# Router weights side by side: two products in place of three for each chunk, and a sum on VectorE

## The chip, the cores and the metric

One core of one Trainium2 chip runs the whole kernel. The metric is the device time of one execution in microseconds (us); lower is better.

## The reference

One decoder layer on 32 sequences of 100 rows with 512 features: self-attention with 16 heads of 128, cross-attention to a context, and a feed-forward layer with a router over 8 experts, of which two add a low-rank term. Only the router matters here. Its logits are the normalised rows times a 512 x 8 matrix:

```python
router_logits = xf @ Wr.T                       # (3200, 512) @ (512, 8)
probs = jax.nn.softmax(router_logits.astype(jnp.float32), axis=-1)
topw, topi = jax.lax.top_k(probs, K)            # K = 2
expert_w = jnp.sum(jax.nn.one_hot(topi, E, dtype=x.dtype) * topw[..., None], axis=1)
...
g_lora = xf @ Ag_e.T @ Bg_e.T * SCALING         # R = 16 columns for each of 8 experts
h = jax.nn.silu(gate_base + g_lora) * (up_base + u_lora)
```

## The kernel before

Products are made in fp16 with split operands. Each fp32 operand is kept as a high half and a low half, and the helper `three` makes one product of three (lines 1553 to 1555): high x high, high x low, low x high, added up in PSUM. Each matmul loads its own stationary operand first (LDWEIGHTS, shown as PEld).

The kernel has a first stage (self-attention, until about 1290 us) in which the weights of the second stage are loaded and split too, in pieces of a fixed order (`B_PIECES`; the router's is number 3 of 17). The second stage goes over groups of five sequences, that is 500 rows in 4 tiles of 125; there are six of them, and a last group of two sequences, 200 rows in 2 tiles of 100. A group has a cross-attention part (`cross_attention`) and a feed-forward part (`layer`), and the order of each engine's work is written out by hand, with semaphores between the engines.

At the end of the cross-attention part of TensorE stand, in this order: the last output products of the group before, the transposes of the normalised rows (`turn_late`, line 1646), the router (`route`), and the low-rank factors (`factors`: 2 x 12 products with as many columns as the group has rows). The layer part follows: `turn_mask` (line 1913) transposes the expert masks, then come the gate and up products in 11 chunks. In the first chunk two more masks are transposed behind the gate products, and the low-rank products wait for the masked factors (`alo`). In the first group nothing stands in front of the router, and three tiles are routed and multiplied by the factors before the fourth is transposed.

In `route` the transposed rows are the stationary operand (125 or 100 columns) and the router's weights are the moving one (8 columns). The results of all tiles of a group lie side by side in one PSUM bank:

```python
for t in range(a, b):
    mm = three(ps[0:tm, 6, t * NE:(t + 1) * NE], [
        (yT_hi[:, e, t * tm:(t + 1) * tm], yT_lo[:, e, t * tm:(t + 1) * tm],
         wr_hi[:, e, :], wr_lo[:, e, :]) for e in range(KC)])
```

On VectorE, `layer` begins with a chain of 16 small instructions (`link`), each of which waits for the one before: the largest logit (line 1459), the subtraction (1460), the first and the second choice (1453 to 1465). Then `spread_out` (1447) writes the first two masks, 16 columns for each expert, four links make the weights, and `spread_out` writes the other two. ScalarE takes two exponentials in between (lines 1004 and 1007; they wait for links 2 and 7). Then VectorE multiplies the factors by the masks (1485, which needs the turned masks of ScalarE, line 1011) and splits the product (1491). Line 1224 is VectorE's half of the split of the transposed rows, which `route` needs.

Of the kernel before, what the change touches and what calls it, by code (L numbers as in the profile page):

```python
# [26 lines left out]
ALU = mybir.AluOpType  # L27
ACT = mybir.ActivationFunctionType
AX = mybir.AxisListType
F32 = mybir.dt.float32  # L30
F16 = mybir.dt.float16
BF16 = mybir.dt.bfloat16

P = 128
S = 100
E = 512
KC = E // P
# [16 lines left out]
NE = 8  # L54
# [51 lines left out]
def decoder_layer(nc, x, wq, wk, wv, wo, q_scale, k_scale, ctxT_in, cwq, cwkv_in, cwo, wg, wu, wd,  # L106
# [8 lines left out]
    with ExitStack() as ctx:  # L115
# [27 lines left out]
        cut = Cut(0)  # L143
# [25 lines left out]
        cut = Cut(w0_at)  # L169
        cwq_hi, cwq_lo = cut([KC, E], F16), cut([KC, E], F16)  # L170
        cwo_hi, cwo_lo = cut([KC, E], F16), cut([KC, E], F16)
        cwkv_hi, cwkv_lo = cut([2 * E], F16), cut([2 * E], F16)
        wr_hi, wr_lo = cut([KC, NE], F16), cut([KC, NE], F16)
        ag_hi, ag_lo = cut([KC, P], F16), cut([KC, P], F16)
        au_hi, au_lo = cut([KC, P], F16), cut([KC, P], F16)
        ad_hi, ad_lo = cut([FC, P], F16), cut([FC, P], F16)
# [12 lines left out]
        cut = Cut(stages_at)  # L189
# [6 lines left out]
        col = {n: cut([NT]) for n in ("m", "d", "r", "m2", "w2")}  # L196
        assert cut.at <= w1_at

        cut = Cut(w1_at)
        yT_hi, yT_lo = cut([KC, GS], F16), cut([KC, GS], F16)  # L200
# [9 lines left out]
        cut = Cut(hb_at + 7687)  # L210
# [11 lines left out]
        cut = Cut(shared_end)  # L222
# [15 lines left out]
        cut = Cut(a_rest)  # L238
# [3 lines left out]
        cut = Cut(hb_at)  # L242
# [217 lines left out]
        def add_piece(src, chunks, width, *parts):  # L460
            B_PIECES.append((src, chunks, width, parts))

        def add_pieces(hi, lo, src, chunks, width):
            step = max(1, 2048 // width)
            src = src.rearrange("(c p) n -> p c n", p=P)
            for a in range(0, chunks, step):
                b = min(chunks, a + step)
                add_piece(src[:, a:b, :], b - a, width,
                          (flat(hi)[:, a * width:b * width], flat(lo)[:, a * width:b * width],
                           0, (b - a) * width))  # L470

        for args in ((cwq_hi, cwq_lo, cwq, KC, E), (cwo_hi, cwo_lo, cwo, KC, E),
                     (cwkv_hi, cwkv_lo, cwkv_in, 1, 2 * E),
                     (wr_hi, wr_lo, wr, KC, NE), (ag_hi, ag_lo, ag, KC, P),
                     (au_hi, au_lo, au, KC, P), (ad_hi, ad_lo, ad, FC, P),
                     (bu_hi, bu_lo, bu, 1, F)):
            add_pieces(*args)
        for hi, lo, w in ((wg_hi, wg_lo, wg), (wu_hi, wu_lo, wu)):
            for e in range(KC):
# [26 lines left out]

            return range(len(B_PIECES))[B_IN_A + b:B_IN_A + b + 1]

        LINKS = 16

        @block.sync
        def _(sp):
# [260 lines left out]
        def _(act):  # L773
# [226 lines left out]
            def layer(g, nb, nxt):  # L1000
                nt, tm = tiles_of(nb)
                gs = nb * S
                act.wait_ge(c["chain"], g * LINKS + 2)
                act.activation(rt["p"][0:tm, 0:nt, :], rt["l"][0:tm, 0:nt, :], ACT.Exp,
                               scale=1 / (X_SCALE * W_SCALE)).then_inc(c["rexp"], 1)
                act.wait_ge(c["chain"], g * LINKS + 7)
                act.activation(col["w2"][0:tm, 0:nt], col["m2"][0:tm, 0:nt], ACT.Exp,
                               scale=1 / (X_SCALE * W_SCALE)).then_inc(c["rexp"], 1)
                def take_mask(k):
                    act.wait_ge(c["mT"], g * 4 + k + 1)  # L1010
                    act.activation(msk[:, k, 0:gs], ps[:, 2 + k % 2, 0:gs],
                                   ACT.Copy).then_inc(c["mTe"], 1)

                take_mask(0)
                take_mask(1)
                for i in range(4):
                    act.wait_ge(c["am"], g * 4 + i + 1)
                    act.activation(am_hi[:, i, 0:gs], tmp[:, i, 0:gs], ACT.Copy).then_inc(c["ahi"], 1)
                    if i % 2:
                        take_mask(2 + i // 2)  # L1020

                def late_hi(k):
                    act.wait_ge(c["late"], 16 * (k + 1 + (k == 2)))
                    for hi, stage, _ in late_parts(k, True):
                        op = act.activation(hi, stage, ACT.Copy, scale=W_SCALE)
                    op.then_inc(c["latehi"], 1)

                def half_h(i, jj):
                    act.wait_ge(c["h"], g * 3 * FC + 3 * jj + i + 1)
                    if i and jj:  # L1030
                        act.wait_ge(c["ad"], g * FC + jj)
                    act.activation(hb_hi[:, jj, 0:gs] if i == 0 else hs_hi[:, i - 1, 0:gs],  # L1032
                                   hh[:, i, 0:gs], ACT.Copy).then_inc(c["hhi"], 1)

                for j in range(FC):
                    act.wait_ge(c["base"], g * 2 * FC + 2 * j + 1)
                    if j:
                        act.wait_ge(c["gs"], g * 2 * FC + 2 * j)
                    act.activation(gb[:, 0:gs], ps[:, 0, 0:gs], ACT.Copy).then_inc(c["gb"], 1)
                    if j:  # L1040
                        act.wait_ge(c["h"], g * 3 * FC + 3 * (j - 1) + 1)
                    act.activation(gate[:, 0, 0:gs], ps[:, 0, 0:gs], ACT.Silu,
                                   scale=1 / (X_SCALE * W_SCALE)).then_inc(c["sg0"], 1)
                    if j:
                        half_h(1, j - 1)
                        half_h(2, j - 1)
                    act.wait_ge(c["base"], g * 2 * FC + 2 * j + 2)
                    if j:
                        act.wait_ge(c["us"], g * 2 * FC + 2 * j)
                    act.activation(ub[:, 0:gs], ps[:, 1, 0:gs], ACT.Copy,  # L1050
                                   scale=H_SCALE / (X_SCALE * W_SCALE)).then_inc(c["ub"], 1)
                    half_h(0, j)
                    for i in (1, 2):
                        act.wait_ge(c["gs"], g * 2 * FC + 2 * j + i)
                        act.activation(gate[:, i, 0:gs], gate[:, i, 0:gs], ACT.Silu,
                                       scale=1 / (X_SCALE * W_SCALE)).then_inc(c["sgs"], 1)
                    if g == 0 and j in LATE_AT:
                        late_hi(LATE_AT[j])
                    if nxt and j == CTX_CHUNK:
                        act.wait_ge(c["alo"], g * 4 + 4)  # L1060
                        context_hi(g + 1, nxt * S)
                half_h(1, FC - 1)
                half_h(2, FC - 1)
                if nxt:
                    cross_attention(g + 1, nxt, nb)
                else:
                    act.wait_ge(c["dsum"], g + 1)
                    act.activation(d_hi[:, 0:gs], tmp[:, 0, 0:gs], ACT.Copy).then_inc(c["dhi"], 1)
# [5 lines left out]
        def _(dve):  # L1074
# [352 lines left out]
            def layer(g, nb, nxt):  # L1427
# [6 lines left out]
                def link(ins):  # L1434
                    ins.then_inc(c["chain"], 1)
                    chain[0] = chain[0] + 1
                    dve.wait_ge(c["chain"], chain[0])

                def wide(name):
                    return col[name][0:tm, 0:nt].unsqueeze(2).to_broadcast([tm, nt, NE])  # L1440

                dve.wait_ge(c["rank"], NE)
                lg, p, a, rest = (rt[n][0:tm, 0:nt, :] for n in "lpab")
                rl = ps[0:tm, 6, 0:nt * NE].rearrange("p (t e) -> p t e", e=NE)

                def spread_out(k):
                    dve.tensor_copy(spread[0:tm, 0:nt, k, :, :],
# [8 lines left out]
                    link(dve.tensor_reduce(col["m"][0:tm, 0:nt], a, AX.X, ALU.max))  # L1456
                    link(dve.tensor_tensor(sel[k][0:tm, 0:nt, :], a, wide("m"), ALU.is_equal))

                link(dve.tensor_reduce(col["m"][0:tm, 0:nt], rl, AX.X, ALU.max))
                link(dve.tensor_tensor(lg, rl, wide("m"), ALU.subtract))  # L1460
                first_of(0, lg)
                link(dve.scalar_tensor_tensor(out=rest, in0=sel[0][0:tm, 0:nt, :], scalar=-1e30,
                                              in1=lg, op0=ALU.mult, op1=ALU.add))
# [82 lines left out]
        def _(pe):  # L1546
            pe.wait_ge(s["ident"], 1)

            def three(out_ap, pairs):

                mm = None
                for i, (ah, al, bh, bl) in enumerate(pairs):
                    pe.matmul(out_ap, ah, bh, start=(i == 0), stop=False)  # L1553
                    pe.matmul(out_ap, ah, bl, start=False, stop=False)  # L1554
                    mm = pe.matmul(out_ap, al, bh, start=False, stop=(i == len(pairs) - 1))  # L1555
                return mm
# [97 lines left out]
            def wide(out_ap, w_hi, w_lo, a, b, gs):  # L1654

                return three(out_ap, [(w_hi[e][:, a:b], w_lo[e][:, a:b],
                                       yT_hi[:, e, 0:gs], yT_lo[:, e, 0:gs]) for e in range(KC)])
# [92 lines left out]
            def cross_attention(g, nb, last_nb):  # L1750
# [117 lines left out]
                def route(a, b):  # L1868

                    mm = None  # L1870
                    pe.wait_ge(c["lnlo"], g * 2 * NT + nt + b)
                    for t in range(a, b):
                        mm = three(ps[0:tm, 6, t * NE:(t + 1) * NE], [
                            (yT_hi[:, e, t * tm:(t + 1) * tm], yT_lo[:, e, t * tm:(t + 1) * tm],
                             wr_hi[:, e, :], wr_lo[:, e, :]) for e in range(KC)])
                    return mm

                def factors(a, b):
# [123 lines left out]
```

## Time and profile before

| | us |
|---|---|
| median of 3 runs | 2565.74 |
| lowest, highest | 2563.83, 2566.78 |
| the profiled execution | 2562.61 |
| its span | 2560.1 |
| TensorE busy (matmuls) | 2459.1 (96%) |
| VectorE busy | 1554.3 (61%) |
| ScalarE busy | 1340.1 (52%) |
| mean granted TensorE clock | 0.981 of 2.4 GHz |

The span runs from the first to the last instruction of the profiled execution; 2.5 us of its time lie around it. An engine's busy time is the union of its instructions. A matmul's own duration contains its latency, so that the sum over matmuls counts time twice where they overlap; the distance between two starts is what one of them costs. The granted clock is what the chip's throttle lets TensorE have: 1.00 is 2.4 GHz, 0.50 is 1.2 GHz.

### The profile page before, as it was taken

How to read it: one execution, taken by the hardware profiler on the slowest of the kernel's cores; microseconds unless marked ns; L12 is line 12 of the kernel's file. 1: busy time of each engine (PE TensorE's matmuls, PEld its weight loads, DVE VectorE, ACT ScalarE, POOL GpSimd, SP SyncE). 2: the span in 40 equal slices, each digit the busy share in tenths (PEclk: the TensorE clock that was granted, in tenths of full speed). 3: DMA queues.
4: the chain of work that ended last, by engine and by line, in shares of the span. 5: the costliest groups of instructions: out<-in, count | busy, mean ns of one | idle time of the engine just before them, and what ended most of it. 6: DMA issues, size and time to landing. Idle time of an engine off the chain costs nothing.

```text
span 2560.1 us, 46046 instructions
## 1 busy us (share of the span) xinstructions
PE 2459.1 (96%) x16474; PEld 1334.5 (52%) x16474; DVE 1554.3 (61%) x3592; ACT 1340.1 (52%) x4109; POOL 844.0 (33%) x794
## 2 busy tenths in 40 slices
PE   6998999999999999999888999999999999999998
PEld 3554554554554555544454465465465465465466
DVE  7777766666566666666545655655655655655644
ACT  4554555555555555565464563563563563564433
POOL 3333333333333333333222422422422422422412
PEclk9999999999999999999969999999999999999999
DMA  5677667777677767798611001001001001001000
GB/s 157 147 175 164 148 151 166 157 166 167 144 164 169 156 154 179 163 187 186 145 63 50 33 18 53 1 18 53 1 18 53 1 17 53 1 18 41 8 17 14
DMA packets 456259, 241.56 MB, mean 94 GB/s; under 512 B 389136, under 2 KB 391824, under 8 KB 455284
## 3 DMA queue, kind: packets, MB, share of 16 engines
q1 hardware_dynamic: 456034, 238.63, 39.8%
q8 instruction: 133, 2.18, 0.4%
q14 instruction: 92, 0.75, 0.1%
HBM read 78.66 MB, written 32.77 MB: 44 GB/s over the span
## 4 chain that ended last, share of the span: by engine, by line
PE 90%; DVE 4%; ACT 3%; issue 2%; POOL 1%; POOLq 0%; ACTq 0%; DVEq 0%
PE ps L1553 25%; PE ps L1555 24%; PE ps L1554 24%; PE ps L1732 3%; PE ps L1733 2%; PE ps L1734 2%; PE ps L1846 2%; ACT mem L974 2%; PE ps L1830 1%; PE ps L1802 1%; PE ps L1742 1%; PE ps L1746 1%; PE ps L1744 1%; PE ps L1824 1%; DVE mem L1224 1%
## 5 line engine op out<-in xcount | busy, mean ns | idle before, releaser
L1553 PE MATMUL ps<-mem 128*128 128x512 f16 (+7 forms) x3992 | 1226.8, 326 | 46.0 <-issue 30.3
L1554 PE MATMUL ps<-mem 128*128 128x512 f16 (+7 forms) x3992 | 1238.2, 325 | 0.0
L1555 PE MATMUL ps<-mem 128*128 128x512 f16 (+7 forms) x3992 | 1222.2, 325 | 0.0
L1553 PEld LDWEIGHTS ps<-mem 128*128 128x128 f16 (+3 forms) x3992 | 413.5, 104 | 372.4 <-issue 51.2
L1555 PEld LDWEIGHTS ps<-mem 128*128 128x128 f16 (+3 forms) x3992 | 414.7, 104 | 316.7 <-issue 9.0
L1554 PEld LDWEIGHTS ps<-mem 128*128 128x128 f16 (+3 forms) x3992 | 416.4, 104 | 305.0 <-issue 8.0
L749 POOL TENSOR_TENSOR mem<-mem 128x500 f32<-128x500 f32 (+1 forms) x231 | 269.2, 1165 | 460.6 <-DVE mem L1505 194.6
L699 POOL TENSOR_TENSOR mem<-mem 128x8 f32<-128x8 f32 x100 | 163.7, 1637 | 510.1 <-DVE mem L1137 510.1
L844 ACT ACTIVATE mem<-ps,mem 100x100 f32<-100x100 f32 x512 | 169.1, 346 | 186.4 <-DVE mem L1167 185.4
L1505 DVE TENSOR_TENSOR mem<-mem 128x500 f16<-128x500 f32 (+1 forms) x231 | 144.7, 650 | 177.0 <-ACT mem L1032 170.8
L711 POOL TENSOR_TENSOR mem<-mem 100x400 f16<-100x400 f32 x128 | 158.5, 1238 | 184.6 <-ACT mem L854 184.6
L824 ACT ACTIVATE mem<-ps 128x512 f32<-128x512 f32 x200 | 117.7, 589 | 169.7 <-DVE mem L1131 85.2
L763 POOL TENSOR_TENSOR mem<-mem 100x400 f32<-100x400 f32 x128 | 107.5, 852 | 290.1 <-DVE mem L1372 290.0
L1032 ACT ACTIVATE mem<-mem 128x500 f16<-128x500 f32 (+1 forms) x231 | 127.9, 585 | 108.2 <-POOL mem L749 108.1
L1198 DVE SCALAR_TENSOR_TENSOR mem<-ps,mem 128x512 f32<-128x512 f32 x100 | 69.0, 690 | 176.3 <-PE ps L1555 176.2
L974 ACT ACTIVATE mem<-ps,mem 100x100 f32<-100x100 f32 x512 | 168.4, 378 | 8.2 <-DVE mem L1351 8.2
L834 ACT ACTIVATE mem<-ps,mem 128x128 f16<-128x128 f32 x400 | 114.0, 368 | 82.8 <-POOL mem L699 82.8
L1131 DVE TENSOR_REDUCE mem<-mem 128x4 f32<-128x512 f32 x200 | 136.1, 681 | 31.6 <-ACT mem L824 31.6
L1516 DVE TENSOR_TENSOR mem<-ps,mem 128x500 f32<-128x500 f32 (+1 forms) x154 | 97.3, 632 | 60.6 <-PE ps L1555 60.2
L705 POOL TENSOR_TENSOR mem<-mem 100x400 f32<-100x400 f32 x128 | 109.1, 852 | 71.9 <-DVE mem L1177 71.9
L1145 DVE SCALAR_TENSOR_TENSOR mem<-ps,mem 128x128 f32<-128x128 f32 x400 | 112.1, 343 | 34.0 <-POOL mem L699 33.8
L974 ACT ACTIVATION_READ_ACCUMULATOR mem<-ps,mem 100x1 f32 x512 | 124.5, 243 | 0.0
(123 smaller groups left out, 3045.5 us busy)
## 6 DMA issues: line engine op xcount, KB each, us to landing
x<-mem SPq DMA_DIRECT2D x100, 256.0 KB, 2.9
mem<-x SPq DMA_DIRECT2D x75, 256.0 KB, 3.7
mem<-in_x SPq DMA_DIRECT2D x50, 256.0 KB, 3.3
mem<-x SPq DMA_DIRECT2D x12, 1000.0 KB
mem<-mem SPq DMA_DIRECT2D x32, 200.0 KB
mem<-mem SPq DMA_DIRECT2D x6, 1000.0 KB
out<-mem SPq DMA_DIRECT2D x6, 1000.0 KB
mem<-in_wq SPq DMA_DIRECT2D x16, 256.0 KB, 4.1
```

The costliest lines, as they stand in the source:

```text
L699: pool.tensor_tensor(rr[:, u % 2, :], ms[:, u % 2, :], half[:, 0:2 * HG], ALU.pow).then_inc(s["rr"], 1)
L711: pool.tensor_tensor(p_split[0:S, n % 2, 1, :, 0:S], probs[0:S, :, :], p_split[0:S, n % 2, 0, :, 0:S], ALU.subtract).then_inc(s["plo"], 1)
L749: pool.tensor_tensor(hh[:, i, 0:gs], gate[:, i, 0:gs], ub[:, 0:gs] if i == 0 else up[:, i - 1, 0:gs], ALU.mult).then_inc(c["h"], 1)
L824: act.activation(sq[:, :, :], bank(kind, u).rearrange("p (h d) -> p h d", d=D), ACT.Square).then_inc(s["sq" + kind], 1)
L844: op = act.activation(probs[0:S, h, :], ps_s[0:S, h * S:(h + 1) * S], ACT.Exp, bias=mx[0:S, h:h + 1], accum_out=den[0:S, h:h + 1])
L974: op = act.activation(cprobs[0:S, i, m, :], ps[0:S, i, m * S:(m + 1) * S], ACT.Exp, bias=cmx[0:S, i, m:m + 1], accum_out=cden[0:S, i, m:m ...
L1032: act.activation(hb_hi[:, jj, 0:gs] if i == 0 else hs_hi[:, i - 1, 0:gs], hh[:, i, 0:gs], ACT.Copy).then_inc(c["hhi"], 1)
L1131: dve.tensor_reduce(ss[:, i, m * HG:(m + 1) * HG], sq[:, :, :], AX.X, ALU.add).then_inc(s["ss"], 1)
L1505: dve.tensor_tensor(lo, hh[:, i, 0:gs], hi, ALU.subtract).then_inc(c["hlo"], 1)
L1553: pe.matmul(out_ap, ah, bh, start=(i == 0), stop=False)
L1554: pe.matmul(out_ap, ah, bl, start=False, stop=False)
L1555: mm = pe.matmul(out_ap, al, bh, start=False, stop=(i == len(pairs) - 1))
```

## The change

The two halves of the router's weights are laid side by side, 16 columns for each chunk. The rows' high half is multiplied by both in one product, the rows' low half by the high half in a second. PSUM then holds two sums of 8 columns for each tile; a new first link on VectorE adds them into `lg`, and the largest logit and the subtraction read `lg` (SBUF) in place of PSUM. The chain has 17 links, and ScalarE waits for one link more. The router's piece keeps its place among the pieces.

```diff
-        wr_hi, wr_lo = cut([KC, NE], F16), cut([KC, NE], F16)
+        wr_both = cut([KC, 2 * NE], F16)
+        wr_hi, wr_lo = wr_both[:, :, 0:NE], wr_both[:, :, NE:2 * NE]
...
-                     (wr_hi, wr_lo, wr, KC, NE), (ag_hi, ag_lo, ag, KC, P),
+                     (ag_hi, ag_lo, ag, KC, P),
...
+            if args[0] is ag_hi:
+                add_piece(wr.rearrange("(c p) n -> p c n", p=P), KC, NE, (wr_hi, wr_lo, 0, KC * NE))
             add_pieces(*args)
...
-        LINKS = 16
+        LINKS = 17
...
-                act.wait_ge(c["chain"], g * LINKS + 2)
+                act.wait_ge(c["chain"], g * LINKS + 3)
...
-                act.wait_ge(c["chain"], g * LINKS + 7)
+                act.wait_ge(c["chain"], g * LINKS + 8)
...
-                rl = ps[0:tm, 6, 0:nt * NE].rearrange("p (t e) -> p t e", e=NE)
+                rl = ps[0:tm, 6, 0:nt * 2 * NE].rearrange("p (t k e) -> p t k e", k=2, e=NE)
...
-                link(dve.tensor_reduce(col["m"][0:tm, 0:nt], rl, AX.X, ALU.max))
-                link(dve.tensor_tensor(lg, rl, wide("m"), ALU.subtract))
+                link(dve.tensor_reduce(lg, rl.rearrange("p t k e -> p t e k"), AX.X, ALU.add))
+                link(dve.tensor_reduce(col["m"][0:tm, 0:nt], lg, AX.X, ALU.max))
+                link(dve.tensor_tensor(lg, lg, wide("m"), ALU.subtract))
...
-                        mm = three(ps[0:tm, 6, t * NE:(t + 1) * NE], [
-                            (yT_hi[:, e, t * tm:(t + 1) * tm], yT_lo[:, e, t * tm:(t + 1) * tm],
-                             wr_hi[:, e, :], wr_lo[:, e, :]) for e in range(KC)])
+                        at = 2 * NE * t
+                        for e in range(KC):
+                            pe.matmul(ps[0:tm, 6, at:at + 2 * NE], yT_hi[:, e, t * tm:(t + 1) * tm],
+                                      wr_both[:, e, :], start=(e == 0), stop=False)
+                            mm = pe.matmul(ps[0:tm, 6, at:at + NE], yT_lo[:, e, t * tm:(t + 1) * tm],
+                                           wr_hi[:, e, :], start=False, stop=(e == KC - 1))
```

## Rows read from the trace of the kernel before

**Rows 1.** The page, busy time of each engine and chain that ended last.

```profile
PE 2459.1 (96%) x16474; PEld 1334.5 (52%) x16474; DVE 1554.3 (61%) x3592; ACT 1340.1 (52%) x4109; POOL 844.0 (33%) x794
...
PE 90%; DVE 4%; ACT 3%; issue 2%; POOL 1%; POOLq 0%; ACTq 0%; DVEq 0%
```

**Rows 2.** TensorE's waits from 1340 us on: total, times, longest.

```profile
PE ps L1553 <- DVE mem L1224: 8.9, 7, 3.3
PE ps L1913 <- DVE mem L1447: 2.5, 2, 1.8
```

**Rows 3.** Timeline of TensorE, group 2: start, length, then the instruction.

```profile
1747.05 0.17 PE L1553 MATMUL ps<-mem 128*125 128x8 f16 x1
...
1749.80 0.37 PE L1553 MATMUL ps<-mem 128*128 128x500 f16 x1
...
1754.88 1.02 PE L1913 MATMUL ps<-mem 125*128 125x125 f32 x8
...
1761.68 0.37 PE L1553 MATMUL ps<-mem 128*128 128x500 f16 x1
```

**Rows 4.** Timeline of VectorE, group 2, with the idle time before.

```profile
1749.97 0.19 DVE L1459 TENSOR_REDUCE mem<-ps 125x4 f32<-125x32 f32 x1 [2.03 <-PE ps L1555]
1750.20 0.19 DVE L1460 TENSOR_TENSOR mem<-ps,mem 125x32 f32<-125x32 f32 x1
...
1752.47 0.76 DVE L1447 COPY mem<-mem 125x512 f32<-125x512 f32 x2
...
1756.61 2.44 DVE L1485 SCALAR_TENSOR_TENSOR mem<-ps,mem 128x500 f32<-128x500 f32 x4 [1.61 <-ACT mem L1011]
1758.96 2.44 DVE L1491 TENSOR_TENSOR mem<-mem 128x500 f16<-128x500 f32 x4
```

**Rows 5.** Group 1: timeline of TensorE; busy times and granted clock (PEclk, third from the end).

```profile
1554.28 0.17 PE L1553 MATMUL ps<-mem 128*125 128x8 f16 x1
...
1557.03 0.37 PE L1553 MATMUL ps<-mem 128*128 128x500 f16 x1
...
1563.79 1.02 PE L1913 MATMUL ps<-mem 125*128 125x125 f32 x8
...
1554.00:1557.40 3.40, 3.40 (x53) 3.08 (x51) 0.88 (x2) 0.00 (x0) 0.00 (x0) 1.00 0.13 42
1557.40:1560.80 3.40, 3.40 (x11) 1.22 (x9) 2.96 (x15) 0.44 (x2) 0.00 (x0) 0.50 0.55 174
```

**Rows 6.** Group 0: timeline of TensorE; one stretch with the granted clock.

```profile
1355.92 0.22 PE L1553 MATMUL ps<-mem 128*125 128x8 f16 x1 [3.26 <-DVE mem L1224]
...
1359.71 0.47 PE L1553 MATMUL ps<-mem 128*128 128x375 f16 x1
...
1362.80 0.36 PE L1554 MATMUL ps<-mem 128*128 128x375 f16 x1
...
1365.07 0.59 PE L1646 MATMUL ps<-mem 125*128 125x125 f32 x4
...
1371.01 1.04 PE L1913 MATMUL ps<-mem 125*128 125x125 f32 x8 [1.76 <-DVE mem L1447]
...
1356.10:1359.50 3.40, 3.40 (x34) 3.40 (x34) 0.22 (x1) 0.00 (x0) 0.00 (x0) 0.50 0.30 128
```

**Rows 7.** Group 6: timeline of TensorE.

```profile
2484.30 0.17 PE L1553 MATMUL ps<-mem 128*100 128x8 f16 x1
...
2485.40 0.25 PE L1553 MATMUL ps<-mem 128*128 128x200 f16 x1
2485.49 0.25 PE L1554 MATMUL ps<-mem 128*128 128x200 f16 x1
...
2488.32 0.53 PE L1913 MATMUL ps<-mem 100*128 100x100 f32 x4 [0.70 <-DVE mem L1447]
```

**Rows 8.** Groups by form, VectorE, reduces: busy, mean ns, idle before.

```profile
L1351 DVE TENSOR_REDUCE mem<-ps 100x4 f32<-100x400 f32 x128 | 66.6, 567 | 64.9 <-PE ps L1830 64.9
...
L1459 DVE TENSOR_REDUCE mem<-ps 125x4 f32<-125x32 f32 x6 | 1.2, 193 | 11.1 <-PE ps L1555 11.1
```

## The prediction

> **What bounds the kernel now.** I read the page first. TensorE is busy 96% of the span and the chain that ended last lies on it for 90% [rows 1]. VectorE is busy 61%: an instruction more on it costs nothing by itself, only where TensorE waits for it. I then asked for TensorE's waits in the stretch that the change touches (1340 us to the end). In seven groups TensorE waited for `spread_out` only twice, 2.5 us in all, and for the row splits of L1224 seven times, 8.9 us [rows 2]. So the router's chain on VectorE is in the open in two groups of seven, and hidden in five. I number the groups 0 to 6; 0 to 5 have four row tiles of 125, and 6 has two of 100. Which is which shows in the timelines of groups 2, 1, 0 and 6, read next.
>
> **Part 1: products removed.** Each row tile had 12 router products (4 chunks of three) and gets 8. That is 16 fewer in each of groups 0 to 5, 8 fewer in group 6, 104 in all. The products overlap, so the cost of one is the distance between starts. In group 2 48 products lie between 1747.05 and 1749.80: 2.75 / 48 = 0.0573 us each [rows 3]. With 100 weight columns it is (2485.40 - 2484.30) / 24 = 0.0458 us [rows 7]. The 25 columns fewer in the weights take 11.5 ns off, so the step follows the load of the weights, not the 8 moving columns, and the 16 columns of the new product should hide under the same load. No row shows 16 columns. Bounds: 0.0573 us again, or the 0.086 us between the two 200-column products of group 6 [rows 7], which would give back 104 x 0.029 = 3.0 us. I take the first; 16 columns are far nearer to 8 than to 200.
>
> The Trainium skill (TensorE: Matmul & The Clock Gate, "Back-to-back issue gap") gives a sustained 81 ns for each load and product pair at 128 columns; by that, the five groups below would give 5 x 16 x 0.081 = 6.5 us, an estimate. The trace has 57 ns and decides.
>
> **Groups 1 to 5.** TensorE has no idle time from the products to the end of the factors, and reaches the first mask transposes (L1913) at 1754.88 [rows 3]. The first two spreads stand complete at 1752.47 + 0.76 = 1753.23 [rows 4]. The slack is 1.65 us. TensorE's 16 x 0.0573 = 0.92 us are therefore kept; the chain ends 0.92 us earlier too, less the new link. The later work moves along: L1485 waits 1.61 us for the masks, which start from L1913 [rows 4]. The split of `am` ends at 1758.96 + 2.44 = 1761.40 and TensorE needs it at 1761.68 [rows 3, 4]. That slack of 0.28 us is small, but both ends count from L1913, so it doesn't change. Five groups: 4.6 us.
>
> **Part 2: one link added.** A TENSOR_REDUCE from PSUM over 64 elements a row. Such a reduce takes 193 ns for 32 elements and 567 ns for 400 [rows 8], so 1.02 ns an element and about 226 ns for 64. The steps of the chain add some 35 ns to an instruction (1749.97 to 1750.20 for the 193 ns one [rows 4]). The link costs 0.26 us (bounds 0.23 and 0.60, by the 32- and the 400-element form); in group 6, with half the elements, 0.24. That L1459 and L1460 read SBUF afterwards in place of PSUM I cost at nothing. In groups 1 to 5 it goes into the slack of 1.65 us and costs nothing; without that cover it would cost 5 x 0.26 = 1.3 us. ScalarE's waits for links 3 and 8 are for the same results as before and move with them.
>
> **Group 0.** Three tiles are routed ahead of the fourth. These 36 products ran from 1355.92 to 1359.71 at the lower clock, 1.2 GHz (granted 0.50), 0.105 us each; 12 fewer are 1.26 us. Of the 24 factor products behind them 10 stepped (1362.80 - 1359.71) / 10 = 0.31 us, and 14 then (1365.07 - 1362.80) / 14 = 0.16 us [rows 6]. If the clock comes back at the same moment, the 1.26 us hold 4 more factor products at the low clock, which would have taken 0.64 us at the high one: 0.64 us gained. If it comes back after the same work, 1.26. I take 0.64. Behind it stand the same fixed waits; nothing else of group 0 is ready too late, since the row transposes at 1365.07 follow without idle time. The last tile saves 4 x 0.057 = 0.23 us in front of a chain that is in the open (TensorE idle 1.76 us until L1447 [rows 6]) and grows by 0.26: -0.03.
>
> The Trainium skill (TensorE: Matmul & The Clock Gate, "What's actually happening") says that warming up costs a span of time and not a number of products, which speaks for 0.64; one trace can't tell the two apart.
>
> **Group 6.** Saved 8 x 0.0458 = 0.37 us, and the chain is in the open here (TensorE idle 0.70 us before L1913 [rows 7]): 0.37 - 0.24 = 0.13 us.
>
> **Part 3: the clock.** In group 1 the router products ran from 1554.28 to 1557.03 with no gap, and then the granted clock was 0.50 from 1557.4 to 1560.8, although TensorE had been busy 3.40 us of the 3.40 before [rows 5]. The factors took 1563.79 - 1557.03 = 6.76 us against 1754.88 - 1749.80 = 5.08 in group 2 [rows 3, 5]: 1.68 us lost. In groups 2 to 5 the same work stayed at 2.4 GHz. What stood before the fall was almost nothing but 8-column products. I read it as: a long enough run of them can cost a step of the clock, and 32 products (1.8 us) in place of 48 (2.75 us) make that rarer. Bounds: 0 and 1.68 us for this execution. I take half, 0.84, since other executions need not have had this fall at all.
>
> **Part 4: no cost.** The weights' split writes the same 32 columns a half, strided, once, in the first stage, in the same place of the order; no queue is passed and no DMA is added.
>
> **The sum.** 4.59 + 0.64 - 0.03 + 0.13 = 5.33 us without the clock, 6.2 us with its half. The profiled execution took 2562.61 us (span 2560.1 and 2.5 around it), 3.1 us under the median of 2565.74; its terms hold for both, but the full clock term (1.68) holds for it alone. The runs of before lie over 2.95 us, about two such falls. Forecast: 2565.74 - 6.2 = 2559.5 us.
>
> **Rivals.**
> - *Products alone.* The clock gives nothing back: 5.33 us, 2560.4. For it: four groups of five had no fall. If 16-column products step a little longer, or the link is longer than thought, it is less: 3.0 us less at the bound, 2563.4. 0.2% of the median, about what a measurement of this kernel can tell from no change, is 5.13 us, so this rival lies on the line. By the Trainium skill (same page and section) the clock falls after an idle stretch, which would leave the fall of group 1 unexplained by the products and make this rival the likeliest; the trace has the fall behind a stretch with no idle time and disagrees. Chance 0.25.
> - *The chain takes the place.* If the time from the products to the masks were set by VectorE, groups 1 to 5 would give 0.92 - 0.26 = 0.66 each, 4.0 us in all, 2561.7. Against: the slack of 1.65 us. Chance 0.05.
> - *Hidden anyway.* Something later in a group (a load, GpSimd) catches up the 0.92 us and only 0.8 us of groups 0 and 6 stay: 2564.9. Against: by line, TensorE's waits after 1340 us that bear on this stretch are 8.9 and 2.5 us, for VectorE's results on data that TensorE itself delivered [rows 2]. Chance 0.05.
> - *More falls of the clock: slower.* Everything after a route comes earlier by a growing amount, so the granted clock may fall where it did not. One fall costs 1.7 us (group 1) or 3.3 (group 0, the low steps until 1362.8 [rows 6]). Once in each of groups 1 to 5, at 2.5 on average: 12.5 - 5.4 = 7.1 us slower, 2572.8. It decides from three such falls on. Against: four groups in this trace had none, with more narrow products. Chance 0.05.
>
> **How the numbers follow.** Forecast 0.60; the rivals as above. Faster by over 0.2%: the forecast with most of its spread (0.55) and a little under half of "products alone": 0.66. Slower 0.04. Within 0.2%: 0.30. The range of 8 in 10: 2556.5 (all of 1.68, 1.26 in group 0 and a further fall gone, 9 us less) to 2563.0 (half of the 16-column bound and no clock term, less the spread of the runs). It takes in "products alone" and "the chain".
>
> **What the profile after would show.** 16-column products with 0.057 us between pairs, and a route of 1.83 us in groups 1 to 5 (0.086 would prove the bound). No idle time before L1913's counterpart in groups 1 to 5; in 0 and 6 idle time of about 1.8 and 0.8 us. A first link of about 0.23 us. Groups 1 to 5 each 0.92 us shorter. The granted clock at 1.00 behind every route of groups 1 to 5. I am wrong if the 16-column products step longer, if a new wait of TensorE appears in the first chunk of a layer, or if the clock falls at new places.

## The result, and the profile after

The changed kernel took 2552.93 us in the median of 7 runs (2549.52 to 2559.04), the kernel before 2565.38 us in the median of 7 (2558.49 to 2566.81). The ratio is 0.9957, with a 95% interval of 0.9943 to 0.9972: 11 us faster, 7 to 15. The forecast said 2559.5 and 6.2 us, with a range from 2556.5. The time fell outside that range, on the fast side. One timed run of the changed kernel (in e5) took 10447.54 us, at a granted clock of 0.557, and counts in no ratio.

The profiled execution took 2550.62 us, span 2548.8, against a span of 2560.1 before: 11.3 us less. The page of the changed kernel, its span and the busy time of each engine, against [rows 1]:

```profile
span 2548.8 us, 45845 instructions
...
PE 2447.8 (96%) x16370; PEld 1326.4 (52%) x16370; DVE 1553.9 (61%) x3599; ACT 1341.1 (53%) x4109; POOL 845.2 (33%) x794
```

TensorE has 104 matmuls fewer (16474 to 16370) and 11.3 us less busy time, VectorE 7 instructions more. The lines have moved by 3 to 7: `three` is at 1557 to 1559, the two products of `route` at 1879 and 1881, the new link at 1462, `spread_out` at 1450, `turn_mask` at 1920.

The timeline of TensorE in group 2, after; it answers to [rows 3]:

```profile
1739.58 0.17 PE L1879 MATMUL ps<-mem 128*125 128x16 f16 x1
1739.61 0.20 PE L1881 MATMUL ps<-mem 128*125 128x8 f16 x1
...
1741.35 0.20 PE L1881 MATMUL ps<-mem 128*125 128x8 f16 x1
1741.40 0.37 PE L1557 MATMUL ps<-mem 128*128 128x500 f16 x1
...
1746.49 1.02 PE L1920 MATMUL ps<-mem 125*128 125x125 f32 x8
```

32 products in 1741.40 - 1739.58 = 1.82 us: 0.057 us each, as with 8 columns. The 16 columns cost nothing. From the first factor product to the masks it is 5.09 us (24 factors; 5.08 before), without idle time: the longer chain is hidden.

The timeline of VectorE in group 2, after; it answers to [rows 4]:

```profile
1741.58 0.23 DVE L1462 TENSOR_REDUCE mem<-ps 125x32 f32<-125x64 f32 x1 [1.11 <-PE ps L1881]
1741.84 0.19 DVE L1463 TENSOR_REDUCE mem<-mem 125x4 f32<-125x32 f32 x1
...
1744.33 0.76 DVE L1450 COPY mem<-mem 125x512 f32<-125x512 f32 x2
...
1748.21 2.44 DVE L1489 SCALAR_TENSOR_TENSOR mem<-ps,mem 128x500 f32<-128x500 f32 x4 [1.36 <-ACT mem L1014]
1750.57 2.44 DVE L1495 TENSOR_TENSOR mem<-mem 128x500 f16<-128x500 f32 x4
```

The link takes 0.23 us and a step of 0.26. The spreads are complete at 1745.09, 1.40 us ahead of the masks (1.65 before), and the idle time in front of L1489 shrinks by the same 0.25 us: that is where the link went.

Group 0, timeline of TensorE, against [rows 6]:

```profile
1351.66 0.23 PE L1879 MATMUL ps<-mem 128*125 128x16 f16 x1 [3.25 <-DVE mem L1227]
...
1354.20 0.47 PE L1557 MATMUL ps<-mem 128*128 128x375 f16 x1
...
1358.54 0.35 PE L1559 MATMUL ps<-mem 128*128 128x375 f16 x1
...
1360.16 0.59 PE L1650 MATMUL ps<-mem 125*128 125x125 f32 x4
...
1366.12 1.04 PE L1920 MATMUL ps<-mem 125*128 125x125 f32 x8 [2.02 <-DVE mem L1450]
```

From the first product to the masks: 14.46 us, before 15.09. That is 0.63 us less, where the prediction had 0.61. In both profiles the low clock lasted until 6.9 us after the first product; 14 factor products fell into it here (to 1358.54) in place of 10.

**Where the 11.3 us are.** I compared the starts of the same instructions in both timelines and followed how far the changed kernel is ahead:

| up to | before, us | after, us | ahead | gained in between |
|---|---|---|---|---|
| first cross-attention product | 1291.20 | 1286.93 | 4.27 | 4.27 |
| first router product, group 0 | 1355.92 | 1351.66 | 4.26 | 0.0 |
| masks, group 0 | 1371.01 | 1366.12 | 4.89 | 0.63 |
| first router product, group 1 | 1554.28 | 1549.41 | 4.87 | 0.0 |
| first router product, group 2 | 1747.05 | 1739.58 | 7.47 | 2.60 |
| first router product, group 3 | 1938.13 | 1929.75 | 8.38 | 0.91 |
| first router product, group 4 | 2129.21 | 2119.91 | 9.30 | 0.92 |
| first router product, group 5 | 2320.30 | 2310.08 | 10.22 | 0.92 |
| masks, group 6 | 2488.32 | 2477.03 | 11.29 | 1.07 |

The 2.60 us up to group 2 are 0.92 us of products and 1.68 us of clock. In group 1 of the changed kernel the granted clock (PEclk, third from the end) is 1.00 from the first router product to the masks, where [rows 5] had the fall:

```profile
1549.40:1556.40 7.00, 7.00 (x58) 4.26 (x57) 5.10 (x22) 0.44 (x2) 0.00 (x0) 1.00 0.36 114
```

Behind the first cross-attention product the changed kernel gains 7.0 us. That is the prediction's sum with the whole of the clock term, 5.33 + 1.68, row by row. The other 4.3 us lie in the first stage, which the change hardly touches. The experiments ask two things: is the fall of the clock in group 1 the work of the router's products, and is the 4.3 us part of the change or of chance?

The second question has a number of its own for each profiled execution: the start of the first cross-attention product, and the span less that start ("behind" below). The granted clock in the first stage before and after, busy times of stretches (PEclk third from the end):

```profile
90.00:220.00 130.00, 122.39 (x785) 63.99 (x784) 97.28 (x235) 68.53 (x212) 45.36 (x44) 0.96 0.74 168
```

```profile
90.00:220.00 130.00, 122.39 (x821) 64.99 (x819) 96.90 (x237) 70.68 (x217) 47.11 (x46) 1.00 0.75 173
```

The first is the kernel before. Its mean of 0.96 over 130 us is 10.4 us at half the clock, up to 5.2 us of time; the changed kernel has none of it there. A little earlier it is the other way round (before, then after):

```profile
50.00:62.00 12.00, 7.56 (x39) 3.76 (x38) 10.75 (x26) 7.26 (x21) 4.97 (x6) 0.86 0.71 158
50.00:62.00 12.00, 7.56 (x33) 3.53 (x32) 9.68 (x24) 6.77 (x18) 4.59 (x6) 0.72 0.72 162
```

There the changed kernel is at half the clock for 3.4 us more, up to 1.7 us of time. So the clock accounts for at most some 3.5 of the 4.3 us. The starts of ScalarE's instructions say the same: the changed kernel is 0.4 us ahead at 18 us, loses 1.5 us at the one fall and gains 1.5, 1.7 and 1.7 us at the three behind it.

### The profile page after: what moved, and what is told of

It reads as the page before. It is cut to its first block, busy times and chain, and to the rows that moved or that the text cites. A ratio compares the mean times of both kernels' runs of the same rounds, so it can differ in the third digit from the quotient of the medians.

```text
span 2548.8 us, 45845 instructions
## 1 busy us (share of the span) xinstructions
PE 2447.8 (96%) x16370; PEld 1326.4 (52%) x16370; DVE 1553.9 (61%) x3599; ACT 1341.1 (53%) x4109; POOL 845.2 (33%) x794
## 4 chain that ended last, share of the span: by engine, by line
PE 89%; DVE 4%; ACT 3%; issue 2%; POOL 1%; DMA 0%; SPq 0%; POOLq 0%; ACTq 0%; DVEq 0%
PE ps L1557 24%; PE ps L1558 24%; PE ps L1559 24%; PE ps L1736 3%; PE ps L1737 2%; PE ps L1738 2%; PE ps L1850 2%; ACT mem L977 2%; PE ps L1834 1%; PE ps L1806 1%; PE ps L1746 1%; PE ps L1750 1%; PE ps L1748 1%; PE ps L1828 1%; DVE mem L1227 1%
## 5 line engine op out<-in xcount | busy, mean ns | idle before, releaser
L1557 PE MATMUL ps<-mem 128*128 128x512 f16 (+4 forms) x3888 | 1206.5, 329 | 41.6 <-issue 30.2
L1558 PE MATMUL ps<-mem 128*128 128x512 f16 (+4 forms) x3888 | 1218.0, 328 | 0.0
L1559 PE MATMUL ps<-mem 128*128 128x512 f16 (+4 forms) x3888 | 1201.7, 328 | 0.0
L1557 PEld LDWEIGHTS ps<-mem 128*128 128x128 f16 (+2 forms) x3888 | 397.9, 102 | 366.1 <-issue 49.6
L1559 PEld LDWEIGHTS ps<-mem 128*128 128x128 f16 (+2 forms) x3888 | 399.1, 103 | 315.4 <-issue 6.4
L1558 PEld LDWEIGHTS ps<-mem 128*128 128x128 f16 (+2 forms) x3888 | 400.8, 103 | 303.5 <-issue 6.1
L1736 PE MATMUL ps<-mem 128*125 128x512 f16 (+1 forms) x312 | 121.4, 389 | 3.2 <-DVE mem L1329 1.9
```

The source lines that it names most:

```text
L1736: pe.matmul(ps[0:tm, 7, :], h_hi, w_hi, start=(j == 0), stop=False)
```

## The experiments

All ratios are to the kernel before, timed beside it on the same chip. Eleven kernels ran.

### e1: the kernel before, again

No edit.

> The kernel before, unchanged. The changed kernel's profiled execution was 11.3 us shorter in its span: 7.0 us behind the router, as the prediction's terms with the whole fall of the clock in group 1 give it, and 4.3 us ahead of any changed product, where the kernel before had three more falls of the granted clock (100 to 260 us). Theory A (chance): where the clock falls in the first stage differs from one execution to the next of the same program, so this one's profile has its first cross-attention product within 5 us of 1295.0 but not always at it, and its ratio to the kernel before is 1.000 with an interval of about 0.15% either way. Theory B (the changed kernel's first stage is systematically shorter): this profile has that product at 1295 again, within 1 us.

Measured: ratio 1.0007 (0.9998 to 1.0016), 2563.47 us in the median of 11 runs against 2561.45 of 27. The same program differs by 11.8 us among its own 38 runs (2557.40 to 2569.21).

First cross-attention product at 1289.94, behind it 1269.06 us (before: 1291.20 and 1268.90). The 1295.0 us of the expectation is a later product of that line, which stands at 1295.03 in the kernel before; the first is at 1291.20, and its counterpart in the changed kernel at 1286.93. This profile alone does not decide: 1289.94 is 1.3 us from the first one. But its clock from 90 to 220 us was 1.00, as in the changed kernel, so falls there come and go with the same program (it had others between 290 and 830 us in their place). And the group 1 stretch was there again, 6.82 us from the last router product to the masks, 5.14 to 5.15 in groups 2 to 5.

### e2: the weights side by side, nothing else

```diff
-        wr_hi, wr_lo = cut([KC, NE], F16), cut([KC, NE], F16)
+        wr_both = cut([KC, 2 * NE], F16)
+        wr_hi, wr_lo = wr_both[:, :, 0:NE], wr_both[:, :, NE:2 * NE]
...
+            if args[0] is ag_hi:
+                add_piece(wr.rearrange("(c p) n -> p c n", p=P), KC, NE, (wr_hi, wr_lo, 0, KC * NE))
```

> The weights' halves side by side and their piece written in that form, but three products of 8 columns and the old chain. If the new place and form of the weights shortens the first stage (theory B), the time falls by about 4 us (ratio 0.9983) and the first stage ends near 1290.8 us. If it costs and brings nothing (theory A), the ratio is 1.000 within 0.1%, the steps between products stay at 0.057 us.

Measured: 1.0004 (0.9995 to 1.0013). First cross-attention product at 1292.51, behind it 1269.09 us. The step between products is 0.0572 us, group 1 again has its 6.82. The layout and its split cost and bring nothing that shows, and they are the only thing that the change does in the first stage.

### e3: the router's products twice

```diff
-                    for t in range(a, b):
+                    for t in [*range(a, b), *range(a, b)]:
```

> The kernel before with every tile's router products made twice (the second time over the first): 96 narrow products in a row in groups 1 to 5, 48 in group 6. By the step between products alone the time grows by 5 x 48 x 0.0573 = 13.8 us in groups 1 to 5, some 1.1 us in group 6 and 0.6 to 3.8 in group 0: 15.5 to 18.7 us. If a long run of narrow products makes the clock fall (theory A), the granted clock is 0.50 behind the products in every group of 1 to 5, and 1.7 us or more comes on top for each, less the one fall that was there: 22 to 30 us, ratio 1.009 to 1.012. If the fall in group 1 had another cause, there is at most one such fall and the ratio is 1.006 to 1.007.

Measured: 1.0136 (1.0121 to 1.0152), some 35 us slower, beyond even the upper figure. Group 1 of this kernel, timeline of TensorE, and then stretches of groups 1 (two) and 2 to 5 with the granted clock:

```profile
1564.07 0.17 PE L1553 MATMUL ps<-mem 128*125 128x8 f16 x1
...
1571.41 0.58 PE L1553 MATMUL ps<-mem 128*128 128x500 f16 x1
...
1577.89 1.02 PE L1913 MATMUL ps<-mem 125*128 125x125 f32 x8
```

```profile
1567.60:1574.30 6.70, 6.70 (x46) 4.84 (x46) 2.34 (x12) 0.44 (x2) 0.00 (x0) 0.50 0.43 145
1560.00:1567.60 7.60, 7.60 (x85) 6.38 (x83) 1.96 (x3) 1.07 (x2) 0.00 (x0) 0.99 0.09 26
1764.00:1771.00 7.00, 7.00 (x57) 4.90 (x57) 2.71 (x13) 0.44 (x2) 0.00 (x0) 0.60 0.43 143
1961.00:1967.00 6.00, 6.00 (x60) 4.25 (x59) 2.28 (x12) 0.44 (x2) 0.00 (x0) 0.72 0.47 153
2156.00:2163.00 7.00, 7.00 (x67) 5.41 (x67) 2.02 (x11) 0.44 (x2) 0.00 (x0) 0.64 0.44 144
2353.00:2360.00 7.00, 7.00 (x70) 5.04 (x70) 2.58 (x13) 0.44 (x2) 0.00 (x0) 0.71 0.38 132
```

By the profile TensorE is busy all of the time in each stretch. This count takes each product's own duration, 0.17 us, though the next one starts after 0.057 us. The clock is at 0.50 for a part of each stretch, so it falls in every group of 1 to 5, where the kernel before has one fall. From the first product to the masks group 1 takes 13.82 us; 96 x 0.0573 + 5.08 = 10.58 would be the time at the full clock. The fall costs 3.2 us here, not 1.7, because it lasts 6.7 us and not 3.4. It comes at 1567.5, before the run of products is over (1571.4); in the kernel before it came 0.4 us behind the run. From the first product to the masks groups 2 to 5 take 13.88, 12.25, 13.87 and 13.93 us, so that the five falls cost some 15 us together. Of the 35 us some 4 more are not products either: 1.8 us between the first cross-attention product and the router of group 0, and 2.2 us between group 0's masks and group 1's router, where the clock was low for longer than in the kernel before.

So with more narrow products the clock falls in each of these groups, with no idle time in the profile. The rival (some other cause of the fall in group 1) would have 1.006 to 1.007.

### e4: the 48 products in two runs

```diff
+                    route(0, nt // 2)
                     some_out(OUT_AFTER[1])
-                    route(0, nt).then_inc(c["rl"], 1)
+                    route(nt // 2, nt).then_inc(c["rl"], 1)
```

> The kernel before with its 48 router products of groups 1 to 5 in two runs of 24, with the 12 wide output products between them. The count of products and the chain are the same. Theory A: no fall of the clock behind the router in any group; the time falls by 1.7 us for each such fall that an execution of the kernel before has, 1 to 2 us (ratio 0.9993), and up to 8 if the kernel before often has one in every group. Rival (the fall in group 1 has nothing to do with the length of the run): no change, and such falls still appear in the profile.

Measured: 0.9994 (0.9985 to 1.0003). The 1.5 us are no more than the noise of the timed runs, but the profile is clear: 5.14 us from the last router product to the masks in groups 1 to 5, group 1 among them, and 1267.55 us behind the first cross-attention product against 1268.90 to 1269.09 in the three with 48 in a row: 1.4 to 1.5 us less. Group 1, from the first router product to the masks:

```profile
1555.90:1566.40 10.50, 10.50 (x87) 6.81 (x86) 6.34 (x23) 1.33 (x4) 0.00 (x0) 1.00 0.22 69
```

The same products, no fall. This execution also had its first cross-attention product at 1295.85, 6 us later than e1's. Nothing of the edit is in front of that product.

### e5 and e9: the changed kernel, two more times

> The changed kernel, unchanged. The fall of the clock in group 1 was there in all three executions profiled with 48 products in a row (1.68 us each), so the whole of it counts, not half: 5.33 + 1.68 = 7.0 us. Theory A (the rest of the first result was the first stage by chance): ratio 0.9973, and the first cross-attention product lies anywhere from 1287 to 1296 us. Theory B (the first stage of the changed kernel is systematically some 4 us shorter): ratio 0.9957, that product near 1287 us again.

> The changed kernel once more. The last call gave 0.9976 (0.9966 to 0.9986) for it and the first result 0.9957 (0.9943 to 0.9972); behind the first cross-attention product the profiled executions of the changed kernel were 7.0 and 7.5 us shorter than that of the kernel before. Theory A: ratio 0.9972 within 0.0010, the same 7 to 7.5 us behind that product, and the product itself between 1287 and 1296 us. Theory B (first stage systematically shorter): ratio near 0.9957.

Measured: e5 0.9976 (0.9966 to 0.9986), e9 0.9975 (0.9965 to 0.9985). Both say 6.1 to 6.4 us, half of what the first seven runs had shown. The spans are 2554.2 and 2547.8 us. The first cross-attention product in the timeline of e5 and of e9:

```profile
1292.73 0.84 PE L1828 MATMUL ps<-mem 100*100 100x400 bf16 x4
```

```profile
1286.28 0.84 PE L1828 MATMUL ps<-mem 100*100 100x400 bf16 x4
```

The same program reaches that product at 1292.73 and at 1286.28, 6.4 us apart; behind it the two take 1261.47 and 1261.52 us, 0.05 apart. Most of the 6.4 us come from one place, a wait of TensorE for a transfer, in e5 and then in e9:

```profile
1142.88 0.24 PE L1557 MATMUL ps<-mem 100*128 100x100 f16 x1 [4.15 <-DMA mem<-mem]
```

```profile
1138.12 0.20 PE L1557 MATMUL ps<-mem 100*128 100x100 f16 x1 [0.32 <-DMA mem<-mem]
```

In e5 the wait is 3.8 us longer, and the clock falls during it (the mean from 1141 to 1150 us is 0.62, which is 6.8 us at half the clock). By ScalarE's starts e9 is 1.0 us ahead in front of this place and 7.6 us right behind it, of which 1.2 us are lost again by 1170. So late data move the first stage too, and not the clock alone. Theory B falls with e5. With e1, e2 and the first profile, the second stage is 1268.90 to 1269.09 us before and 1261.47 to 1261.87 after.

### e6: without the new link

The largest logit and the subtraction read the first 8 columns of PSUM. The product of the rows' high half and the weights' low half is made and left out of the logits.

```diff
-                link(dve.tensor_reduce(lg, rl.rearrange("p t k e -> p t e k"), AX.X, ALU.add))
-                link(dve.tensor_reduce(col["m"][0:tm, 0:nt], lg, AX.X, ALU.max))
-                link(dve.tensor_tensor(lg, lg, wide("m"), ALU.subtract))
+                rh = rl[:, :, 0, :]
+                link(dve.tensor_reduce(col["m"][0:tm, 0:nt], rh, AX.X, ALU.max))
+                link(dve.tensor_tensor(lg, rh, wide("m"), ALU.subtract))
```

> The changed kernel without the new link: the largest logit and the subtraction read the first 8 columns of PSUM, so the product of the rows' high half and the weights' low half is made and left out of the logits. Prediction's sum: the link is hidden in groups 1 to 5 and in the open in 0 and 6, so 0.26 + 0.24 = 0.5 us less than the changed kernel, TensorE's idle time before the first masks 1.76 us again in place of 2.02 in group 0 and 0.7 in place of 0.9 in group 6. Rival (the chain sets groups 1 to 5 too): 1.8 us less, and the stretch from the last router product to the first masks shorter than 5.14 us there.

Measured: 0.9973 (0.9963 to 0.9984); the changed kernel beside it had 0.9976. TensorE's wait for `spread_out`, total, times and longest, in e5 and then in e6:

```profile
PE ps L1920 <- DVE mem L1450: 2.9, 2, 2.0
```

```profile
PE ps L1920 <- DVE mem L1450: 2.5, 2, 1.8
```

Two waits in both, 0.4 us less in all without the link. From the last router product to the masks it is 5.14 to 5.15 in groups 1 to 5 with and without it. Behind the first cross-attention product: 1261.16 against 1261.47 us. From the first router product to the masks, group 0 takes 14.10 us against 14.37 and group 6 3.65 against 3.87: 0.49 us, as forecast. The link costs 0.3 to 0.5 us a kernel.

### e7: the changed kernel in two runs of 16

The same edit as e4 on the changed kernel.

> The changed kernel with its 32 router products in two runs of 16 around the wide output products. Theory A: the clock already stays up behind 32, so nothing is left to gain: ratio to the changed kernel 1.000 and the stretch behind the route 5.14 us in groups 1 to 5. Rival: runs of 32 still cost a fall in some executions, then this one is 1 to 2 us faster than the changed kernel.

Measured: 0.9981 (0.9972 to 0.9989), with 1262.38 us behind the first cross-attention product: nothing gained. The changed kernel's groups 1 to 5 have no fall left to remove (5.14 us in all of them, in all three of its profiles). In group 0, whose products the edit does not touch, the clock fell 2.0 us behind the first product here and not with it, and the stretch to the masks took 12.88 us in place of 14.4 to 14.5: the gain of group 0 depends on when its fall comes.

### e8, e10 and e11: 128 weight columns

The row tiles are the stationary operand, 125 columns wide. e8 loads 128 columns of the changed kernel's tiles where the next tile's rows stand behind (all but the last of a route); the three more rows fall into PSUM rows that nobody reads. e10 does this to the kernel before, e11 to the last tile of a full group too, with four columns of room behind the rows.

```diff
+                        tw = P if t + 1 < b else tm
                         for e in range(KC):
-                            pe.matmul(ps[0:tm, 6, at:at + 2 * NE], yT_hi[:, e, t * tm:(t + 1) * tm],
+                            pe.matmul(ps[0:tw, 6, at:at + 2 * NE], yT_hi[:, e, t * tm:t * tm + tw],
```

```diff
-        yT_hi, yT_lo = cut([KC, GS], F16), cut([KC, GS], F16)
+        yT_hi, yT_lo = cut([KC, GS + 4], F16), cut([KC, GS + 4], F16)
...
-                        tw = P if t + 1 < b else tm
+                        tw = P if t + 1 < b or t == NT - 1 else tm
```

> The changed kernel with 128 weight columns in place of 125 or 100 for every tile but a group's last (the three more rows of the next tile land in unused PSUM rows). If the step between narrow products follows the number of weight columns alone, it grows from 0.0571 to 0.0584 us and the time by 24 x 0.0013 x 5 = 0.15 us, ratio to the changed kernel 1.000. If a full load of 128 columns is the quicker one (it lasts 0.10 us against 0.14 in the trace of the kernel before), the step falls to 0.03 to 0.05 us: 24 x 0.007 to 0.027 = 0.2 to 0.65 us in each of groups 1 to 5, 1 to 3.3 us in all.

> The kernel before (three products of 8 columns, no new link) with 128 weight columns for every tile but a group's last. The step fell to 0.0325 us with 128 columns in the changed kernel. Here 36 products of 48 get it: 36 x 0.0247 = 0.89 us in each of groups 1 to 5, and the run of narrow products lasts 1.86 us as in the changed kernel, so no fall of the clock in group 1: 4.4 + 1.7 + about 0.8 for groups 0 and 6 = 6.9 us, ratio 0.9973. If the fall depends on the number of narrow products and not on how long they last, it stays, and the ratio is 0.9980.

> The changed kernel with 128 weight columns for the last tile of a full group too (four columns of room behind the rows). Eight more products of a group step 0.0325 in place of 0.057 us: 0.2 us in each of groups 1 to 5 and as much in group 0 in front of the open chain, 1.2 us less than with the other tiles alone, about 11.5 us less than the kernel before behind the first cross-attention product, ratio 0.9955.

Measured: e8 0.9966 (0.9954 to 0.9977), e10 0.9966 (0.9954 to 0.9978), e11 0.9944 (0.9931 to 0.9956), 2547.58 us in the median.

Group 2 of e8, timeline of TensorE:

```profile
1739.70 0.17 PE L1880 MATMUL ps<-mem 128*128 128x16 f16 x1
...
1740.31 0.20 PE L1880 MATMUL ps<-mem 128*125 128x16 f16 x1
...
1740.77 0.37 PE L1557 MATMUL ps<-mem 128*128 128x500 f16 x1
```

24 products with 128 weight columns take 1740.31 - 1739.70 = 0.61 us, 0.025 each; 8 with 125 take 0.46 us, 0.057 each. Three columns more make a narrow product more than twice as fast. My expectation for e10 and e11 took 0.0325 for it, which is the mean over both kinds, and so was too small. Behind the first cross-attention product e10 has 1259.52 us (9.4 to 9.6 less than before, expected 6.9) and e11 1255.13 (13.8 to 14.0 less, expected 11.5).

The Trainium skill (TensorE: Matmul & The Clock Gate, "Weight-path perf modes — Fast Weight Load (FWL) and DoubleRow") says that a fast load of weights is used when there are exactly 128 of them and they are not fp32; these runs agree, 0.025 us against 0.057. The prediction did not draw on it.

These three totals contain accidents of one execution. The time from the first router product of a group to its masks does not; in each of groups 1 to 5 it is:

| | us |
|---|---|
| before (groups 2 to 5) | 7.83 to 7.84 |
| changed (after, e5, e9) | 6.91 |
| e10: before, 36 of 48 products with 128 columns | 6.68 |
| e8: changed, 24 of 32 with 128 columns | 6.15 |
| e11: changed, all with 128 columns | 5.86 |

So the padding is worth 1.15 us a group to the kernel before, more than the change (0.92 us). With the quick load the change is still worth 0.53 us a group (6.68 less 6.15), or 2.6 us in five groups, although e8 and e10 have the same ratio and lie only 1.1 us apart behind the first cross-attention product. Two accidents hide it. e8's profiled execution (and e11's) had one more fall of the clock, at the masks of group 0, and e8's took 184.84 us from there to group 1's router, where both kernels of the first result took 183.3. From 1362 to 1372 us its mean granted clock was 0.83:

```profile
1362.00:1372.00 10.00, 7.98 (x58) 5.56 (x58) 8.31 (x27) 3.75 (x8) 0.00 (x0) 0.83 0.14 53
```

And e10 took 70.87 us behind the masks of group 6, the kernel before 71.78.

e10 also answers its second question. Its 48 products last 1.6 us, and its clock stays at 1.00 in group 1: at the same number of narrow products the fall went with how long they lasted. That is one execution.

e11 is the fastest version measured, but its edit does two things. The four columns of room also change the distance between the rows of `yT`, which the factor, gate and up products read. The 128x500 products of group 2 step 211.2 ns in e11 and 211.9 in e8 (mean of 493 steps each), and from a group's masks to the next router it takes 182.91 us in place of 183.26. That is 0.35 us a group that the padding of the last tile did not bring. The spacing alone was not tried.

## Why the prediction was right, and where its range was wrong

- **The products.** 0.0573 us each forecast, 0.057 measured for 16 and 8 columns alike; 0.92 us a group forecast, 0.91 to 0.92 measured in groups 2 to 5. The bound of 0.086 us did not apply.
- **The link.** 0.26 us forecast, 0.26 measured; hidden in five groups (e6). The idle time before the masks grew to 2.02 us in group 0 and 0.92 in group 6; the prediction named 1.8 and 0.8, though by its own sum the link comes on top of 1.76 and 0.70.
- **Group 0.** 0.61 us forecast, 0.63 measured. The low clock ended at the same time behind the first product, not behind the same number of products, as the term assumed. Both executions had the fall right at the first product; in two of the thirteen profiles (e3, e7) it came 2.0 us later.
- **The clock term was under-sized.** The prediction took half of 1.68 us because the fall in group 1 might be an accident of one execution. It is not: all three profiled executions with the 48 products in a row (before, e1, e2) have it, in group 1 and there alone, and none of the nine whose runs of narrow products are shorter in time has it (the first one after and e4 to e11). In e4 the run was broken up and the fall was gone; in e3 it was doubled and each group had a fall. The term of 0.84 us measured 1.68, and the sum is 7.0 us.
- **The rivals.** "Products alone" gave 5.33 us; the profiles have 7.0 to 7.6 behind the first cross-attention product. The timed runs cannot decide this: the interval of e5, 0.9966 to 0.9986, is 3.6 to 8.7 us. "The chain takes the place" and "hidden anyway" are excluded by the unchanged stretch from the products to the masks and by the table. More falls at new places did not come in groups 1 to 5 of any profile of the changed kernel.
- **The step that failed** is the range: "2556.5 (all of 1.68, 1.26 in group 0 and a further fall gone, 9 us less)". It took a fall or two of the clock as all the chance that there is, and gave the first stage no term. Part 4 put the change's cost there at nothing, which e2 bears out; but the first stage moves by itself. With one and the same program it ends anywhere from 1286.3 to 1292.7 us (e5, e9), and 1289.9 to 1295.9 with the kernel before's code (e1, e4). In the first result's profiles it brought 4.3 of the 11.3 us. The forecast was also set against one median of three runs, 2565.74; the medians of the same kernel beside the experiments were 2561.45, 2562.06 and 2562.79.

So the size of the first result, 11 us, is luck on top of a gain that is real. Repeated twice the difference was 6.1 and 6.4 us. That these lie so near to the forecast of 6.2 says little, since their intervals hold 7.0 as well, and the profiles say 7.0 to 7.6.

Which of the first stage's many waits end in a fall, and why an execution has more or fewer, was not tested, nor why e5's transfer came late. I have no reason for the fall's place in group 1 alone. Two of the three profiles of the changed kernel are 0.4 us shorter behind the first cross-attention product than the first; 0.2 to 0.3 us of it lie ahead of group 0's router and 0.1 us in group 0, and the cause is open.

## What to carry to other kernels

Cost a stream of narrow matmuls by the distance between their starts, and look at what sets it: here it was the load of the weights, so that twice the moving columns were free and three more weight columns (125 to 128) were worth more, 1.15 us a group in e10, than the removal of a third of the products, 0.92 us. Here a run of narrow products lowered TensorE's clock for itself and for the wide ones behind it, although the profile shows no idle time; look at the granted clock during and behind each such run. Wide products in between (e4) and a shorter run (the change, e10) each avoided it here. And before you explain a difference of a few tenths of a per cent, run the same program twice, compare from a fixed instruction behind the unsteady part, and go by the stretch that the edit touches, since one fall elsewhere (e8) can hide a gain of the same size.

## What the runs showed of the hardware that was not expected

- Narrow products with 128 weight columns step 0.025 us, with 125 columns 0.057 us, in the same stream (e8).
- The granted clock fell to 0.50 with TensorE busy by the profile in every moment before: once behind 48 products of 8 columns (cost 1.7 us; before, e1, e2), in each of five groups with 96 (e3; cost 3.2 us in group 1). It never fell in groups 1 to 5 with 32 products, with two runs of 24 and 12 wide products between them (e4), or with 48 that lasted 1.6 us (e10).
- Identical programs end their first stage 6.4 us apart (1286.28 and 1292.73) and take the same time behind it within 0.05 us (1261.52 and 1261.47). One wait for a transfer, 4.15 us against 0.32, stands in the middle of the difference.
